# Attention pipelined by halves of the queries, sums by two transposes and a compact reciprocal, and a ring of ten tiles in the first FFN

## What is computed

```python
x = x + attn_a(layernorm(x))   # 16 heads of 16, rotary, causal softmax(q k^T / 4) v, then Wo
x = x + ffn(layernorm(x))      # silu(x Wg) * (x Wu) -> Wd, 256 -> 768 -> 256, int weights / 127
x = x + attn_b(layernorm(x))   # RWKV-6 style recurrence, 4 heads of 64
x = x + ffn(layernorm(x))
```

## Time and profile before

| | us |
|---|---|
| median of 3 runs | 3503.28 |
| profiled execution, its own time | 3503.35 |
| its span, first to last instruction | 3501.6 |
| TensorE busy | 3000.5 (86%) |
| VectorE (DVE) busy | 2487.5 (71%) |
| ScalarE (ACT) busy | 1311.2 (37%) |
| GpSimd (POOL) busy | 1307.0 (37%) |

### The profile page before, as it was taken

One profiled execution on the slowest core, in us unless ns is written; L12 is line 12 of the kernel. 1 busy time (PEld: TensorE's weight loads), 2 busy tenths in 40 slices (PEclk: granted clock), 3 DMA queues, 4 the chain that ended last, 5 costly groups with the idle time before them and its releaser, 6 DMA issues.

```text
span 3501.6 us, 47094 instructions
## 1 busy us (share of the span) xinstructions
PE 3000.5 (86%) x17056; PEld 1850.4 (53%) x17056; DVE 2487.5 (71%) x5137; ACT 1311.2 (37%) x2721; POOL 1307.0 (37%) x1244
## 2 busy tenths in 40 slices
PE   2488989889889888889888898898988889898898
PEld 1236565365743567345763457635565355653667
DVE  4675787667775677856878568775687757876565
ACT  0264223622336322453225531265313643236322
POOL 0023551235512454124631347213462235522455
PEclk9699999999999999899998999899998999999999
DMA  3600032000510006000150002400023000330000
GB/s 130 110 2 13 19 64 54 2 13 19 79 39 13 2 19 98 20 14 10 29 97 2 14 10 46 80 2 13 19 46 71 2 13 19 52 66 2 1 1 13
DMA packets 68885, 115.01 MB, mean 33 GB/s; under 512 B 10795, under 2 KB 64075, under 8 KB 65531
## 3 DMA queue, kind: packets, MB, share of 16 engines
q1 hardware_dynamic: 68627, 111.51, 16.2%
HBM read 74.69 MB, written 33.65 MB: 31 GB/s over the span
## 4 chain that ended last, share of the span: by engine, by line
PE 46%; DVE 32%; POOL 9%; issue 5%; ACT 4%; DMA 2%; SPq 0%; DVEq 0%; ACTq 0%; POOLq 0%
DVE mxp L967 9%; PE PB L1311 7%; PE PB L1296 5%; PE PB L1386 5%; PE PB L1371 5%; PE PB L1282 4%; DVE arena L1156 4%; PE PB L1425 3%; PE PB L1344 3%; DVE arena L1165 2%; PE PB L1460 2%; DVE attn L890 2%; ACT arena L722 2%; PE PB L1450 2%; DVE stats L879 1%
## 5 line engine op out<-in xcount | busy, mean ns | idle before, releaser
L967 DVE TENSOR_REDUCE mxp<-PB 128x1 f32<-128x512 f32 (+3 forms) x1536 | 752.9, 549 | 160.8 <-PE PB L1282 87.1
L722 ACT ACTIVATE arena<-PB 128x512 f32<-128x512 f32 (+3 forms) x1536 | 650.5, 508 | 455.5 <-PE PB L1296 450.6
L1282 PE MATMUL PB<-arena 96*128 96x512 bf16 (+3 forms) x1536 | 513.0, 362 | 106.7 <-DVE mxp L967 64.3
L582 POOL TENSOR_SCALAR_AFFINE_SELECT arena<-arena 128x512 f32<-128x512 f32 x256 | 163.5, 639 | 1003.7 <-ACT arena L722 1003.3
L1296 PE MATMUL PB<-arena 99*128 99x512 bf16 (+3 forms) x1536 | 467.7, 344 | 26.5 <-DMA arena<-augT 19.3
L1282 PEld LDWEIGHTS PB<-arena 96*128 96x128 bf16 x1536 | 154.8, 102 | 428.0 <-DVE mxp L967 326.1
L1311 PE MATMUL PB<-arena 128*32 128x512 f32 (+3 forms) x3072 | 339.9, 515 | 15.5 <-ACT attn L711 13.7
L1371 PE MATMUL PB<-xh,wgu 128*128 128x512 f32 x768 | 313.7, 408 | 42.3 <-DVE xl L1034 29.0
L592 POOL TENSOR_TENSOR hl<-arena,hh 128x512 fp32r<-128x512 f32 x192 | 248.3, 1293 | 262.3 <-ACT hh L747 256.9
L1371 PE MATMUL PB<-xl,wgu 128*128 128x512 f32 x768 | 309.6, 403 | 2.8 <-issue 2.8
L1555 PE MATMUL PB<-arena 128*128 128x128 f32 x1792 | 235.4, 283 | 56.1 <-DVE arena L1156 46.7
(11 more groups left out here) (139 smaller groups left out, 5372.6 us busy)
## 6 DMA issues: line engine op xcount, KB each, us to landing
arena<-parts SPq DMA_DIRECT2D x112, 256.0 KB, 9.7
parts<-arena SPq DMA_DIRECT2D x192, 128.0 KB
arena<-parts SPq DMA_DIRECT2D x16, 768.0 KB, 18.4
arena<-in_x SPq DMA_DIRECT2D x16, 512.0 KB, 4.5
arena<-parts SPq DMA_DIRECT2D x16, 512.0 KB, 21.0
xres<-in_x SPq DMA_DIRECT2D x16, 512.0 KB, 4.8
out<-xres SPq DMA_DIRECT2D x16, 512.0 KB, 3.4
wgu<-arena SPq DMA_DIRECT2D x2, 768.0 KB, 4.5
```

What stands on the lines that cost most here:

```text
L582: pool.affine_select(out=a, in_=a, compare_op=ALU.is_ge, fill=0.0, base=0, pattern=[[0, HG], [1, 128]], channel_multiplier=-1).then_inc(ma ...
L722: act.activation(pt[:, U % 3, h, 0:n], bank(b, "score", t)[:, 0:n], ACT.Exp, scale=DH ** -0.5).then_inc(act_emptied, 1)
L967: dve.reduce_max(mxp[:, g % 2, h, col:col + 1], bank(b, "max", g * NPC + k)[:, 0:n], axis=AX.X).then_inc(dve_emptied, 1)
L1282: last = mm(ps[:, 0:n], qst[0:AUG, h, 128 * i:128 * i + 128], kst[0:AUG, h, s0:s0 + n], start=True, stop=not diag)
```

## The change

1. The second pass takes the units of the first half of the queries (4) before those of the second (8). The maxima are ordered in blocks by half too (11 and 27 pieces a group: narrow pieces of two or four heads share one bank and one reduction), 152 a sequence in place of 192. The splitting of a block's maximum moves to POOL (`max_parts`), once for each half. A table made at build time (`score_steps`) sets how many scores follow each piece: none for the first 25, then 0.6, and from piece 52 on 1.27.
2. `den` goes by halves, in three instructions: the second transpose reads the reciprocal with a stride of zero, and the widening copy and its tile are gone.
3. `out_proj` of the first two banks stands inside the scores of the last group, that of the last two behind the first hidden tile of the FFN.
4. The first FFN's tiles move to the room of `qst` and `kst`; its rings have ten tiles, the second half's transposes stand ahead of tile 4, the first down projection ahead of tile 8. The second FFN stays as it was.
5. `qst`, `kst` and their DRAM copies are laid out half by half.

```diff
 def score_units():
 
-    return [(j, f) for j in range(NT) for f in (0, 1) if 128 * j < HALF * (f + 1)]
+    return [(j, f) for f in (0, 1) for j in range(4 * f + 4)]
 
 
 def max_pieces():
 
     out = []
-    for i in range(NT):
-        out.append((i, 0, min(HALF, 128 * (i + 1)), i))
-        if i >= 4:
-            out.append((i, HALF, 128 * (i + 1) - HALF, NT + i - 4))
+    for f in (0, 1):
+        if f:
+            out.append([((h,), i, 0, HALF, i) for i in range(4, NT) for h in range(HG)])
+        else:
+            out.append([])
+        for a in (3, 2, 1, 0):
+            n = 128 * (a + 1)
+            heads = [(h,) for h in range(HG)] if a >= 2 else [(0, 1), (2, 3)] if a else [tuple(range(HG))]
+            out[f] += [(hs, 4 * f + a, HALF * f, n, 4 * f + a + 4 * f) for hs in heads]
     return out
 
 
@@ -49,25 +54,59 @@
 
...
+MAXES = [(k, p) for k in range(2 * NG) for p in PIECES[k % 2]]
+BLOCK_END = [max(t for t, (k, _) in enumerate(MAXES) if k == q) for q in range(2 * NG)]
+LAST_UNIT = [len(UNITS) * (k // 2) + (len(UNITS) - 1 if k % 2 else 3) for k in range(2 * NG)]
 KV_ORDER = [0, 2, 1, 3]
-DOWN_AT = 6
-V_AT = (8, 20)
-SLOTS = 7
+DOWN_AT = {1: 4, 3: 6}
+SECOND_AT = {1: 4, 3: 2}
+V_AT = (4, 8)
+SLOTS = {1: 10, 3: 7}
...
+NMAX = len(MAXES)
+NSC = NG * HG * len(UNITS)
+LAG = 15
+AUG_AT = 5
+
+
+def score_steps():
+
+    done, credit, out = 0, 0.0, []
+    for t in range(NMAX):
+        ready = [k for k in range(2 * NG - 1) if t >= BLOCK_END[k] + LAG]
+        most = HG * (LAST_UNIT[ready[-1]] + 1) if ready else 0
+        credit = min(credit + (1.27 if t >= BLOCK_END[1] + LAG else 0.6), 2.0)
+        n = max(0, min(int(credit), most - done))
+        credit -= n
+        done += n
+        out.append(done)
+    while done < NSC:
+        done = min(NSC, HG * (done // HG + 1))
+        out.append(done)
+    return out
+
+
+DONE = score_steps()
+STEPS = len(DONE)
+
+
+def step_of(s):
+
+    return next(t for t, n in enumerate(DONE) if n > s)
+
+
+AUG_STEP = [min(BLOCK_END[k] + AUG_AT, NMAX + 1) for k in range(2 * NG)]
+UNIT_STEP = [step_of(HG * U + HG - 1) for U in range(NG * len(UNITS))]
+OUT_AFTER = [LAST_UNIT[k] + (3 if k < 2 * NG - 2 else 2) for k in range(2 * NG)]
+DEN_STEP = [UNIT_STEP[OUT_AFTER[k]] + 4 for k in range(2 * NG - 2)]
+O_STEP = UNIT_STEP[NG * len(UNITS) - 4]
...
+        def ffn_tiles(k, first, hidden):
+            return (rounded(f"xh{k}", first, [128, NC, T]), rounded(f"xl{k}", first + 2048, [128, NC, T]),
+                    region(first + 4096, 512 * TURNS).rearrange("p (r t) -> p r t", r=TURNS),
+                    rounded(f"hh{k}", hidden, [128, SLOTS[k], HALF]),
+                    rounded(f"hl{k}", hidden + 512 * SLOTS[k], [128, SLOTS[k], HALF]))
+
+        ffn_sets = {1: ffn_tiles(1, 0, 4096 + 512 * TURNS), 3: ffn_tiles(3, HIGH, HIGH + 4096 + 512 * TURNS)}
...
-                    for g in range(NG):
-                        wait_emptied(sp, b, "aug", g)
-                        for r in range(3):
-                            sp.dma_start(qst[AUG + r:AUG + r + 1, HG * g:HG * g + HG, :],
-                                         augT[32 * r:32 * r + 32, g % 2, :]).then_inc(aug_loaded[g], 16)
+                    for k in range(2 * NG):
+                        g, f = k // 2, k % 2
+                        wait_emptied(sp, b, "aug", k)
+                        sp.dma_start(qst[AUG:AUG + 3, f, HG * g:HG * g + HG, :], augT[:, k % 2, :]).then_inc(aug_loaded[k], 16)
...
+                    def max_parts(k):
+                        m = mxp[:, k // 2 % 2, :, 4 * (k % 2):4 * (k % 2) + 4]
+                        parts_ = [aug[:, k % 2, r, :, :] for r in range(3)]
...
+                        pool.tensor_scalar(parts_[0], m, -1.0, 1.0, ALU.mult, ALU.mult).then_inc(aug_chain, 1)
+                        pool.tensor_tensor(augf[:, :, :], m, parts_[0], ALU.add).then_inc(aug_chain, 1)
+                        pool.tensor_scalar(parts_[1], augf[:, :, :], -1.0, 1.0, ALU.mult, ALU.mult).then_inc(aug_chain, 1)
+                        pool.tensor_tensor(augf[:, :, :], augf[:, :, :], parts_[1], ALU.add).then_inc(aug_chain, 1)
+                        pool.tensor_scalar(parts_[2], augf[:, :, :], -1.0, 1.0, ALU.mult, ALU.mult).then_inc(aug_chain, 1)
...
+                    for t in range(STEPS):
+                        if t in BLOCK_END:
+                            max_parts(BLOCK_END.index(t))
+                        for U in DIAG_UNITS:
+                            if UNIT_STEP[U] == t:
+                                mask_unit(U)
+                        if t in DEN_STEP:
+                            over_sums(DEN_STEP.index(t))
+                        if t == O_STEP:
+                            over_sums(2 * NG - 2)
                     ln_scale(1, b, 0)
-                    ln_scale(1, b, 1)
+                    over_sums(2 * NG - 1)
...
+                    def den(k):
+                        g, f = k // 2, k % 2
...
+                        dve.transpose(sums, attn[:, 4 * f:4 * f + 4, g, :]).then_inc(den_chain, 1)
+                        one = recip[:, f, :].rearrange("p (a n) -> p a n", n=1)
+                        dve.reciprocal(one, sumT[:, f, :].rearrange("p (a n) -> p a n", n=32)[:, :, DH:DH + 1]).then_inc(den_chain, 1)
+                        dve.transpose(sumT[:, f, :].rearrange("p (a n) -> p a n", n=32),
+                                      one.broadcast_to([128, HALF // 32, 32])).then_inc(den_chain, 1)
...
+                    for t in range(STEPS):
+                        if t < NMAX:
+                            max_piece(t)
+                        if t in BLOCK_END[1::2]:
+                            join_max(BLOCK_END.index(t) // 2)
+                        if t in AUG_STEP:
+                            aug_out(AUG_STEP.index(t))
+                        if t in DEN_STEP:
+                            den(DEN_STEP.index(t))
+                    den(2 * NG - 2)
...
+                    dve.wait_ge(x_loaded[0], 16 * (b + 1))
+                    residual("o", 0, 0)
+                    residual("o", 1, 0)
+                    ln_half(1, 0)
+                    den(2 * NG - 1)
+                    x_low(1, 0, (0, 1))
...
-                            if e == 2:
+                            if e == SECOND_AT[k]:
                                 x_low(k, s, (2, 3))
-                                if k == 1 and ahead:
-                                    x0_means(b + 1, 0)
-                            if e == NM + DOWN_AT // 2:
+                            if e == 5 and k == 1 and ahead:
+                                x0_means(b + 1, 0)
+                            if e == 1 and k == 1:
+                                dve.wait_ge(x_loaded[1], 16 * (b + 1))
+                                residual("o", 2, 0)
+                                residual("o", 3, 0)
+                                ln_means(1, b, 1, stats, mv)
+                            if e == 2 and k == 1:
+                                ln_norm(1, b, 1, xres, xn, mv, rstd)
+                            if e == NM + DOWN_AT[k] // 2:
                                 down(k, 0)
                                 down(k, 1)
                                 if k == 1:
                                     ln_means(2, b, 0, stats, mv)
                             gate(k, s, e)
...
+                    def out_proj(n):
+                        wait_bank(pe, b, "o", n)
+                        pe.wait_ge(attn_normed, 8 * b + 2 * NG - 1 + n // 2)
+                        for a in (0, 1):
+                            for g in range(NG):
+                                last = mm(bank(b, "o", n)[:, D * a:D * a + D], attn[:, 2 * n + a, g, :], wo[:, g, :],
+                                          start=(g == 0), stop=(g == NG - 1))
+                        last.then_inc(filled, 1)
+
+                    for t in range(STEPS):
+                        if t < NMAX:
+                            if t in (0, BLOCK_END[3] + 1):
+                                pe.wait_ge(stacked[1 if t else 0], 9 * 16 * (b + 1))
+                            max_item(t)
                         if t in V_AT:
                             v_item(b, 2 + V_AT.index(t))
...
+                        if t in AUG_STEP:
+                            k = AUG_STEP.index(t)
+                            pe.wait_ge(aug_chain, 40 * b + 5 * k + 5)
+                            wait_bank(pe, b, "aug", k)
+                            pe.transpose(bank(b, "aug", k)[0:48, 0:64].bitcast(bf16),
+                                         aug[:, k % 2, :, :, :].rearrange("p r h i -> p (r h i)"), identb[:, :]).then_inc(filled, 1)
+                        for s in scores_of(t):
+                            U = s // HG
+                            if s % HG == 0 and UNITS[U % len(UNITS)][0] == 0:
+                                k = 2 * (U // len(UNITS)) + UNITS[U % len(UNITS)][1]
+                                pe.wait_ge(aug_loaded[k], 16 * (b + 1))
```

(32 more changed lines are left out.)

312 lines of the change are left out of this document (126 added, 186 removed).

## The result

The change takes 3473.33 us (median of 5 runs, 3469.49 to 3485.58), the kernel before beside it 3499.93 (5 runs, 3498.15 to 3503.86): a ratio of 0.9927 (0.9907 to 0.9947), so 26.6 us less. The forecast was 3483. The profiled execution took 3469.49 us, its span is 3467.7.

A forecast was written before the change was run, and what follows sets the result against it. No engine is full; TensorE and DVE, both nearly full, wait for each other through six banks. 4.3 us less a sequence, 8 x 4.3 = 34, less 14 in the first, gives 20: 3483 us from 3503.35; range 3430 to 3545.

The forecast's parts named there:

- First 52 pieces: Start of a sequence's attention, DVE taking maxima with few scores beside it: piece 52 comes at 35.0 us.
- From there to the last maximum: Pieces 52 to 151 with 125 scores, 31.25 units: 79.3 us, or 2.54 a unit; maxima end at 114.3.
- the attention's halves alone bring 7.0: Claim that the maxima end 7.0 us earlier in a sequence, credited to splitting attention by halves of the queries.
- five `den` of 1.5: Reciprocal stops on DVE between scores, about 1.5 us each, mostly covered by the ring of banks; 2.9 us counted.
- The end of attention: Last maximum to last `pv`, with `out_proj` of two banks and the wait for `over_sums`: 37.1 us against 29.2.
- The gap: Last `pv` to the FFN, with scale, normalization, `den` and two subtractions: 5.3 us in place of 18.5.
- The FFN: First FFN to the second half's down projection: 31.2 plus 13.5, so 44.7 us in place of 36.7.
- The ring of ten takes the wait away: First FFN: ten tiles remove tile 7's wait for its place, but a fourth tile and the normalization stay.
- Program: Whole run: 8 x 4.3 = 34 us, less 14 in the first sequence, is 20 us less: 3483 us.
- case 2: Rival: the two passes run freer at 2.36 us a unit, 45 us less, 3438; chance 0.18.
- case 3: Rival: tighter pairing starves TensorE or DVE; break-even at 2.62 a unit, at 2.76 55 us more, 3538; chance 0.20.
- case 4: Rival: clock falls at the end of attention after TensorE idles at `over_sums`; 6 us more a sequence, 3531; chance 0.10.

The follow-up runs named there:

- e9: The kernel before with the compact reciprocal alone (three `den` steps, no widening copy): 3462.44 us, 0.9889 of the kernel before.
- e6: The change with `max_parts`, whole, moved from POOL to DVE: 3547.84 us, 1.0129 of the kernel before.
- e5: The change with the widening copy of `den` put back, four steps a half: 3510.53 us, 1.0024 of the kernel before.
- e10: e9 with the split of a group's maxima on POOL as well: 3462.40 us, 0.9893 of the kernel before.
- e11: e2 with the copy to augT on ACT and, in the first sequence, the second load of x issued later: 3427.28 us, 0.9791 of the kernel before.
- e2: The change with `over_sums` on POOL ahead of the mask of the unit just issued: 3428.52 us, 0.9800 of the kernel before.
- e8: The change without TensorE's conditional branch ahead of the first FFN: 3480.37 us, 0.9934 of the kernel before.
- e4: The change with the first FFN's ring cut from ten tiles to seven: 3478.90 us, 0.9939 of the kernel before.
- e12: e11 with the first FFN's first down projection one tile later, ahead of tile 9: 3407.74 us, 0.9735 of the kernel before.

## Why the prediction was right, point by point

The forecast's path held: attention gains ahead of the last maximum, loses behind it, and what `out_proj` saves comes back in the FFN. Its sizes held less well. Means of the second to the eighth sequence, the change against the kernel before:

| stage | forecast | measured |
|---|---|---|
| to the last maximum | 7.0 less | 8.8 less (113.9 for 122.7) |
| end of attention | 7.9 more | 5.8 more (34.9 for 29.1) |
| gap | 13.2 less | 12.3 less (6.2 for 18.5) |
| FFN to the second down projection | 8.0 more | 10.6 more (47.4 for 36.8) |
| together | 4.3 less | 4.7 less (202.3 for 207.0) |

The first two are better than forecast by 3.9 us, the last two worse by 3.5. That the sum fits to 0.4 us is luck.

- **First 52 pieces:** 35.0 forecast, 32.8 measured (33.5 in the second and eighth sequence). Eight reductions of 512 columns take 4.87 us, so 0.61 each where 0.63 was counted, the join takes 0.19 and not 0.6, and less is left of the other small terms. Four reductions of 128 elements in one instruction go at the speed of one (0.69 us), as assumed.
- **From there to the last maximum:** 79.3 forecast, 80.8 measured, so 2.59 us a unit for 2.54. It is nearer to 2.62, at which the forecast breaks even, than to the forecast; what was too long before hides it, and the last maximum comes at 113.6 for 114.3.
- **The cause of that gain** was put wrongly: "the attention's halves alone bring 7.0". The compact reciprocal alone brings 4.3 of the 8.8 us (e9, 118.4), and the rest comes with the other edits, which weren't tried apart, and only with the split on POOL: with it on DVE the last maximum comes at 122.5 (e6), as late as before.
- **DVE's small stops.** The forecast let 2.9 us show of five `den` of 1.5. What is put on DVE in the busy passes shows in full (e5: 2.3 us for 2.2; e6: 5.3 for 4.9), and where the clock falls behind it, about twice (e5: 4.8). What is taken off DVE brings as much only where TensorE waited for it and no other wait takes over: so in e9, not in e10 and e11. DVE's reductions aren't slowed by the split on POOL: 682 ns on average beside it, 678 where POOL stands idle, so the sum was right to add nothing.
- **The end of attention:** 37.1 forecast, 34.6 measured in the fifth sequence (36.2 in the fourth). The way from the last maximum to the exps is 2.3 (3.1 forecast), the wait at `over_sums` 5.0 with its clock (e2; 2.1 and 1.0 forecast). The rest, ACT's drain of the group and the last units, is then 3.6 less than counted.
- **The gap:** 5.3, measured 6.0 to 6.5. What was missing is TensorE's branch, which `out_proj` hid before (e8).
- **The FFN:** 44.7 forecast, measured 47.0 in the fifth sequence. To the end of the first down projection it was to be 31.2 and is 34.1: the two waits of TensorE there, 0.87 us for the normalization and 2.36 for `hl`, weren't in the sum. From there on 13.5 were forecast, 12.9 measured. "The ring of ten takes the wait away" is wrong in what it suggests: with seven tiles nothing is lost either (e4). The place of the down projection is what costs (e12).
- **Program:** seven times 4.7 less 9.7 in the first sequence (as forecast) is 23 us, 20 forecast. The profiled executions differ by 33.9, the medians by 26.6. What wasn't forecast is the rest of each sequence, whose code stays but for the load of `x0`: 2.2 us shorter in the second to the seventh (217.3 to 215.1), 1.3 and 1.0 us longer in the first and the eighth, 11 in all. About 1.0 of the 2.2 is the last down projections of the first FFN, which ran at a lower clock before. About 1.0 lies in the recurrence.

There two subtractions of DVE take a microsecond less; before, and in the change:

```profile
1701.47 2.45 DVE L1156 TENSOR_TENSOR arena<-arena 64x512 f32<-64x512 f32 x2
2113.67 1.45 DVE L1219 TENSOR_TENSOR arena<-arena 64x512 f32<-64x512 f32 x2
```

The second of the two lasts 1.67 us where it starts some 0.3 us behind POOL's instruction, 0.69 where it starts 0.2 to 0.4 us ahead of it, in the first seven sequences of every trace here. The short one stands also in e9's sixth sequence (rest 215.2, the others 217.1 to 217.4), whose code there is the kernel before's, and it is missing in the change's seventh (216.1). So this part is a matter of how the instructions happen to fall, and no gain of the change.

The rivals: with 2.59 us a unit the passes don't run freer (case 2 is out), and they are slower than forecast but stay short of 2.62, where the loss of case 3 begins. The clock falls at `out_proj` in all eight sequences, but costs 1.4 to 3.0 us instead of 6 (case 4 in part).

The whole, against the kernel before: the compact reciprocal alone 38.7 us less (e9), the change without it nothing (e5). Everything else in the change thus costs some 12 us as it stands. With the order of `over_sums` and the mask turned (e2) the same edits take 31 off e9 by the ratios, and with the down projection where it was before, 54 (e12, which has e11's edits too). Two places in an order held back more than the change gained.

## What to carry to other kernels

Before you take work off an engine that empties the banks, ask of each piece whether TensorE waits for it there, and what it will wait for instead: 0.43 us of each `den` held it up in full (e5), eight copies held up nothing (e11), and a split moved to another engine was only waited for there (e10). Price each stop of TensorE with the slower matmuls that may follow: in e9 the faster ones are two thirds of the gain ahead of the last maximum. When instructions are put into another stream's gap, read on every engine what stands ahead of them there: here one mask ahead of `over_sums` ate more than the whole change gained. Time the parts one by one, since a good part can pay for bad ones.
